# Storing the second attention's query and key parts in another layout, two key heads in the projection and the others from inside the attention

## The reference, cut to what matters

```
qkv = x @ Wqkv                                        # x: 2 x 1024 x 128
q = qkv[..., :256].reshape(B, 32, S, 8)               # 32 query heads of 8 features
k = qkv[..., 256:320].reshape(B, 8, S, 8)             # 8 key heads
v = qkv[..., 320:].reshape(B, 8, S, 8)
scores = q @ k.T / sqrt(8), masked causally, softmax  # 4 query heads share one key head
```

## Time and profile before

| | us |
|---|---|
| median of 3 runs (lowest, highest) | 3863.41 (3859.98, 3866.43) |
| the profiled execution, its own time | 3872.14 |
| its span, first to last instruction | 3870.2 |
| PE busy | 3113.8 |
| DVE busy | 2241.5 |
| ACT busy | 2093.1 |
| POOL busy | 1068.2 |
| mean granted TensorE clock | 0.899 |

### The profile page before, as it was taken

The page is one execution under the profiler, slowest core; times in us unless marked ns, Lnnn a source line. Parts: engine busy times, 40 slices in busy tenths (PEclk is TensorE's granted clock), DMA queues, the critical chain, the costliest instruction groups (busy, mean ns, idle before and its releaser), DMA issues. The chain is left out here.

```text
span 3870.2 us, 73056 instructions
## 1 busy us (share of the span) xinstructions
PE 3113.8 (80%) x24437; PEld 1669.6 (43%) x24437; DVE 2241.5 (58%) x3754; ACT 2093.1 (54%) x3805; POOL 1068.2 (28%) x967
## 2 busy tenths in 40 slices
PE   2787885279505999991999999999999999999997
PEld 1332331123201333331565566556556556655653
DVE  6888886732415777775555555555554554555553
ACT  1477775012201666660666666666666666666664
POOL 0000000024102111111554344344344434434540
PEclk7689778589755999995999999999999999999998
DMA  5221113034271111114111111111111111111111
GB/s 192 86 76 59 64 63 102 1 82 107 43 37 22 26 25 25 25 25 125 41 52 33 46 37 48 40 44 47 30 50 38 47 40 40 51 30 50 41 34 40
DMA packets 191919, 199.74 MB, mean 52 GB/s; under 512 B 113781, under 2 KB 120581, under 8 KB 186794
## 3 DMA queue, kind: packets, MB, share of 16 engines
q1 hardware_dynamic: 154218, 193.05, 18.1%
q10 hardware_dynamic: 37344, 1.97, 1.0%
HBM read 99.64 MB, written 28.97 MB: 33 GB/s over the span
## 5 line engine op out<-in xcount | busy, mean ns | idle before, releaser
L2398 POOL TENSOR_TENSOR tr_t<-tr_t 128x512 f32<-128x512 f32 x384 | 488.4, 1272 | 705.8 <-DVE tr_t L2242 705.8
L2405 POOL TENSOR_TENSOR tr_nq<-tr_t,tr_rn 128x512 f32<-128x512 f32 x384 | 392.2, 1043 | 395.2 <-ACT tr_rn L2138 395.2
L1610 DVE TENSOR_REDUCE attn_mp<-attn_ps 128x1 f32<-128x512 f32 (+3 forms) x660 | 395.6, 657 | 163.7 <-PE attn_ps L1461 86.5
L2103 ACT ACTIVATE tr_pr<-tr_ps 128x768 f32<-128x768 f32 x264 | 213.9, 810 | 375.1 <-PE tr_ps L1925 374.8
L2241 DVE TENSOR_TENSOR tr_t<-tr_ps,tr_tab 128x512 f32<-128x512 f32 x384 | 263.4, 686 | 242.7 <-ACT tr_sq L2112 242.6
L1940 PE MATMUL tr_ps<-tr_w,tr_xs 128*128 128x512 f32 x768 | 371.2, 605 | 32.1 <-DVE tr_xs L2269 27.9
L1572 ACT ACTIVATE attn_pr<-attn_ps 128x768 f32<-128x768 f32 (+2 forms) x352 | 300.9, 870 | 168.4 <-PE attn_ps L1494 165.5
L2251 DVE TENSOR_TENSOR tr_o<-tr_ps,tr_rd 128x384 f32<-128x384 f32 (+1 forms) x264 | 144.1, 546 | 427.8 <-ACT tr_rd L2128 426.9
L684 DVE TENSOR_REDUCE attn_mcol<-attn_ps 128x1 f32<-128x512 f32 x548 | 358.1, 683 | 46.3 <-PE attn_ps L529 36.7
L668 ACT ACTIVATE attn_pr<-attn_ps 128x512 f32<-128x512 f32 x512 | 272.7, 600 | 88.6 <-DVE attn_ps L706 69.0
L1925 PE MATMUL tr_ps<-tr_qT,tr_kT 64*128 64x96 f32 (+1 forms) x4224 | 300.9, 282 | 0.0
(11 more groups left out here) (260 smaller groups left out, 4947.3 us busy)
## 6 DMA issues: line engine op xcount, KB each, us to landing
tr_v<-tr_va SPq DMA_DIRECT2D x144, 192.0 KB, 2.5
attn_ka<-scratch_kp SPq DMA_DIRECT2D x72, 294.0 KB
tr_v<-tr_va SPq DMA_DIRECT2D x144, 128.0 KB, 2.4
moe_cb<-scratch_combineT SPq DMA_DIRECT2D x32, 512.0 KB
tr_w<-in_w_half SPq DMA_DIRECT2D x12, 1024.0 KB
tr_v<-tr_va SPq DMA_DIRECT2D x48, 256.0 KB, 2.4
scratch_kp<-proj_parts SPq DMA_DIRECT2D x36, 256.0 KB
attn_km<-scratch_kp SPq DMA_DIRECT2D x72, 98.0 KB
```

Of the source, the lines that this page charges most:

```text
L1610: dve.tensor_reduce(dst, src, AX.X, ALU.max).then_inc(maxed, 1)
L2398: pool.tensor_tensor(t12[:, slot, i, 0, :], t12[:, slot, i, 0, :], t12[:, slot, i, 1, :], ALU.add).then_inc(summed, 1)
L2405: pool.tensor_tensor(nq[:, slot, i, :].rearrange("p (h e) -> p h e", e=DH), t12[:, slot, i, 0, :].rearrange("p (h e) -> p h e", e=DH), rn[ ...
```

## The change

The layout of the scratch tensors changes: a key head's 128 tokens are now kept as pieces of 128 tokens (256 bytes), ordered by feature group. `move_q` writes one key head's query parts of one column tile by three DMAs, `move_k` its key parts by three, so nine DMAs (`MOVES`) write one key head. The projection writes heads 0 (SP) and 1 (ACT queue) only. `parts` lives on through the attention, with 512 columns of zeros behind its 2048 tokens; the attention's SP writes heads 2 and 3 before its loop and head `kv + 4` in iteration `kv`, and loads head `kv + 3` there (the third head, 2, before the loop), after the first output store. The stores of ones in `stage_masks` go. The loads of queries read rows of 32 pieces of 128 bytes where they read one run of 4 KB. POOL's copies read the new order. ACT's two copies of the output sums move from after a = 4 and a = 15 to after a = 3 and a = 14.

```diff
 def stage_masks
-            for h in range(2):
-                sp.dma_start(d["k1"][:, :, B * NK1 + h, :]...)
-            for h in range(2 * QPK):
-                sp.dma_start(d["q1"][:, :, B * NQ1 + h, :]...)
-            sp.wait_ge(stored, 16 * (3 + 2 * QPK))
+            sp.wait_ge(stored, 16)
+AHEAD = 4
+FIRST = 2
+MOVES = 9
+def move_q(eng, d, parts, kv, ct, signal):
+    for part in range(3):
+        dst = d["q1"][part, :, bass.ds(kv, 1), ct * 16 * P:(ct + 1) * 16 * P]
+        eng.dma_start(dst.rearrange("e o (c t) -> c e (o t)", t=P), parts[:, ct, part, bass.ds(kv * P, P)]
+                      ).then_inc(signal, 16)
+def move_k(eng, d, parts, kv, signal):
+    for part in range(3):
+        dst = d["k1"][part, :, bass.ds(kv, 1), :]
+        eng.dma_start(dst.rearrange("e o (c t) -> c e (o t)", t=P), parts[0:NK1 * HD, 2, part, bass.ds(kv * P, P)]
+                      ).then_inc(signal, 16)
 def stage_project1        # SP; the ACT queue the same with head 1
             for ct in range(2):
                 sp.wait_ge(split_done, ct + 1)
-                n += store_q(sp, ct, range(0, 8), stored)
+                move_q(sp, d, parts, 0, ct, stored)
             sp.wait_ge(split_done, 3)
-            n += store_k(sp, range(0, 4), stored)
-            sp.wait_ge(stored, 16 * n)
+            move_k(sp, d, parts, 0, stored)
+            sp.wait_ge(stored, 16 * MOVES)
...
             dve.memset(vaug[:], 1.0).then_inc(ones_ready, 1)
+            dve.memset(parts[:, :, :, T:], 0.0)
 def stage_attention1      # SP
-                    heads = bass.ds(kv * QPK + 2 * half, PAIRS)
-                    n += load_packed(sp, qh[halves[half], slot % 2], d["q1"][:, :, heads, :], QPART1, loaded[slot])
+                    heads = d["q1"][:, :, bass.ds(kv, 1), :].rearrange("a e o (c x) -> a e (o c) x", x=P)
+                    n += load_packed(sp, qh[halves[half], slot % 2], heads[:, :, :, 64 * half:64 * half + 64], QPART1,
+                                     loaded[slot])
...
             load(1, 1)
+            for kv in range(FIRST, AHEAD):
+                for ct in range(2):
+                    move_q(sp, d, parts, kv, ct, moved[kv % 2])
+                move_k(sp, d, parts, kv, moved[kv % 2])
+            sp.wait_ge(turned, 5)
+            sp.wait_ge(moved[0], 16 * MOVES)
+            load(2, 2)
...
-                    sp.wait_ge(qk_done, kv * UNITS + 1)
-                    load(kv + 2, (s + 2) % 4)
                     sp.wait_ge(out_copied, 2 * kv + 1)
                     store(QPK * kv + 1, 0)
+                    sp.wait_ge(turned, 5 * kv + 10)
+                    sp.wait_ge(moved[(s + 1) % 2], 16 * MOVES * (2 * i + (s + 3) // 2))
+                    load(kv + 3, (s + 3) % 4)
+                    for ct in range(2):
+                        move_q(sp, d, parts, kv + AHEAD, ct, moved[s % 2])
+                    move_k(sp, d, parts, kv + AHEAD, moved[s % 2])
                     sp.wait_ge(out_copied, 2 * kv + 2)
                     store(QPK * kv + OROW, 1)
 # POOL: the same five copies per head (turn_piece), reading the new order, at HEADS_AT = 8 of its list
-                                 kp[:, slot % 2, :].rearrange("p (j c t) -> p j t c", c=8, t=16)
+                                 kp[:, slot % 2, :].rearrange("p (c j t) -> p j t c", c=8, t=16)
-                        src = qh[:, slot % 2, p, :].rearrange("p (c m o t) -> p o m c t", c=32, o=2, t=4)
+                src = qh[:, slot % 2, :, :].rearrange("p c (h m o t) -> p h o m c t", h=2, o=2, t=4)
 # ACT
-                        if a == 4:
+                        if a == 3:
                             copy_out(2 * kv, 0, kv)
-                        elif a == 15:
+                        elif a == 14:
                             copy_out(2 * kv + 1, 1, kv)
 SCRATCH
-    "q1": ([3, HD, (B * NK1 + 2) * QPK, S], BF16),
-    "k1": ([3, HD, B * NK1 + 2, S], BF16),
+    "q1": ([3, HD, B * NK1 + AHEAD, QPK * S], BF16),
+    "k1": ([3, HD, B * NK1 + AHEAD, S], BF16),
```

More of the change, by code:

```diff
@@ L1091, in _, with stage_project1 @@
             dve.tensor_copy(negmask[:], m[:])
-def stage_project1(nc, d, xnT, vaug):
+AHEAD = 4
[11 more added lines that the diff above has]
+                      ).then_inc(signal, 16)
+def stage_project1(nc, d, xnT, vaug, parts):
     with Stage(nc, "proj1") as st:
         w = st.sb("w", [P, 2 * D + 2 * NK1 * HD])
-        parts = st.sb("parts", [P, 3, 3, T], BF16)
         r0, r1, r2 = st.sb("r0", [P, 3, T]), st.sb("r1", [P, T]), st.sb("r2", [P, T])
@@ L1111, in stage_project1 @@
         NV = NK1 * HD
[L1113 to L1129, removed]
         @block.sync
@@ L1177, in _ @@
                     k += 1
-            n = 0
             for ct in range(2):
                 act.wait_ge(split_done, ct + 1)
-                n += store_q(act, ct, range(8, 16), copied)
+                move_q(act, d, parts, 1, ct, copied)
             act.wait_ge(split_done, 3)
-            n += store_k(act, range(4, 8), copied)
-            act.wait_ge(copied, 16 * n)
+            move_k(act, d, parts, 1, copied)
+            act.wait_ge(copied, 16 * MOVES)
         @block.vector
@@ L1189, in _ @@
             dve.memset(vaug[:], 1.0).then_inc(ones_ready, 1)
+            dve.memset(parts[:, :, :, T:], 0.0)
             for j, rows in enumerate((P, P, NV)):
                 dve.wait_ge(mm_used, NC * (j + 1))
-                split_parts(link, dve, r0[0:rows, j, :], parts[0:rows, j, 0, :], parts[0:rows, j, 1, :],
-                            parts[0:rows, j, 2, :], r1[0:rows, :], r2[0:rows, :])
+                split_parts(link, dve, r0[0:rows, j, :], parts[0:rows, j, 0, 0:T], parts[0:rows, j, 1, 0:T],
+                            parts[0:rows, j, 2, 0:T], r1[0:rows, :], r2[0:rows, :])
                 dve.sem_inc(split_done, 1)
@@ L1215 @@
 LEAD_STEPS = 8
+HEADS_AT = 8
 PAIRS = 2
@@ L1294, in unit_index, with stage_attention1 @@
     return pos if pos < STEP_POS[T_STEP] else pos - 1
-def stage_attention1(nc, d, vaug, ident, identb, negmask):
+def stage_attention1(nc, d, vaug, parts, ident, identb, negmask):
     NKH = B * NK1
@@ L1303, in stage_attention1 @@
     with Stage(nc, "attn1") as st:
-        qh = st.sb("qh", [P, 2, PAIRS, S], BF16)
+        qh = st.sb("qh", [P, 2, 32, PAIRS * 32], BF16)
         kp = st.sb("kp", [P, 2, S], BF16)
@@ L1324, in stage_attention1 @@
         pool_begun = st.sem("pool_begun")
+        moved = [st.sem("moved0"), st.sem("moved1")]
         block = st.block()
@@ L1378, in _, with turn_keys, turn_queries, turn_piece @@
             for slot in range(4):
-                sp.wait_ge(loaded[slot], 16 * NLOAD * (NKH // 4 + (1 if slot < 2 else 0)))
+                sp.wait_ge(loaded[slot], 16 * NLOAD * (NKH // 4 + (1 if slot < 3 else 0)))
+            for x in range(2):
+                sp.wait_ge(moved[x], 16 * MOVES * (NKH + AHEAD - FIRST) // 2)
         @block.gpsimd
         def _(pool):
-            def turn_heads(slot):
+            def turn_keys(slot):
                 pool.tensor_copy(kh[:, slot, :].rearrange("p (j t c) -> p j t c", t=16, c=8),
-                                 kp[:, slot % 2, :].rearrange("p (j c t) -> p j t c", c=8, t=16)).then_inc(turned, 1)
-                for p in range(PAIRS):
-                    for c in range(2):
-                        src = qh[:, slot % 2, p, :].rearrange("p (c m o t) -> p o m c t", c=32, o=2, t=4)
-                        pool.tensor_copy(qt[:, slot, p, c * 4:c * 4 + 4, :].rearrange("p m (c t) -> p m c t", t=4),
-                                         src[:, c]).then_inc(turned, 1)
+                                 kp[:, slot % 2, :].rearrange("p (c j t) -> p j t c", c=8, t=16)).then_inc(turned, 1)
+            def turn_queries(slot, p, c):
+                src = qh[:, slot % 2, :, :].rearrange("p c (h m o t) -> p h o m c t", h=2, o=2, t=4)
+                pool.tensor_copy(qt[:, slot, p, c * 4:c * 4 + 4, :].rearrange("p m (c t) -> p m c t", t=4),
+                                 src[:, p, c]).then_inc(turned, 1)
+            def turn_piece(slot, i):
+                if i == 0:
+                    turn_keys(slot)
+                else:
+                    turn_queries(slot, (i - 1) // 2, (i - 1) % 2)
             def copy_values(kv, slot):
@@ L1403, in _ @@
                 pool.wait_ge(loaded[slot], 16 * NLOAD)
-                turn_heads(slot)
+                for x in range(5):
+                    turn_piece(slot, x)
             copy_values(0, 0)
@@ L1413, in _ @@
                             copy_values(kv + 1, (s + 1) % 2)
-                        if a == 10:
+                        if a == HEADS_AT:
                             pool.wait_ge(loaded[(s + 2) % 4], 16 * NLOAD * (i + 1 + (1 if s >= 2 else 0)))
                             pool.sem_inc(pool_begun, 1)
-                            turn_heads((s + 2) % 4)
+                            for x in range(5):
+                                turn_piece((s + 2) % 4, x)
         @block.tensor
```

10 lines of the change are left out of this document (3 added, 7 removed).

## The result

The changed kernel takes 3755.44 us (3748.00 to 3762.12, four runs) against 3864.92 (3859.98 to 3875.91, four runs): a ratio of 0.9712, 95% interval 0.9684 to 0.9741, 109.5 us less. The forecast was 3750 us, 113.5 us less.

The account below looks back on a forecast made before the run. Stores, through their number of pieces, bound an idle 96.7 us stretch; in the attention's loop PE is busy and waits for ACT's copy. Terms -4.05, -92, +0.5 and -18 give 113.5 us less: 3750 us, range 3738 to 3778.

Parts of the forecast that it names:

- Masks: Masks stage: ten stores go, so the next stage's load goes out 4.05 us sooner (3.8 to 4.3).
- Projection: Projection's end: 120 stores in 73,728 pieces give way to 18 stores; the attention starts 92 us sooner (90.9 to 93.6).
- Padding memset: Zeros behind the tokens in the projection: 4.1 us on DVE, costing nothing because DVE stands idle 14.29 us there.
- First loads: Attention's start: load 0 now reads 3072 pieces of 128 bytes; +0.5 us, bounds 0 to 5.9.
- SP's budget: Attention's loop: loads and moves before the second store take 10.1 us of 14.6 allowed, so PE does not wait.
- M: SP's nine moves in a head of the attention's loop: 4.0 us taken, from 3.0 to 6.2.
- signs of being right: Listed profile signs, among them SP idle before its second store and no PE wait for the row maxima's DMA.
- The copies: Attention's loop: ACT's two earlier copies remove PE's waits of 1.24 us a head; 18 us saved, at most 19.8.
- rival B: Attention's loop: PE's waits only move to the later exponential or DVE's maxima; 3768 us, chance 0.17.
- C: Attention's loads: small pieces at 2.87 ns hold up SP, rows 2.6 us late a head; 3797 us, chance 0.07.
- E: Projection's end held by something other than piece count, such as a fixed store cost; 20 us tail gives 3770, chance 0.03.
- D: Attention's two-part query loads run on few DMA engines, making the kernel slower than before; 3941 us, chance 0.03.

Follow-up runs that it names:

- the run with whole rows: First mention: kernel before, its 120 stores writing rows as 4 KB runs, 3785.73 us; second: changed kernel, loaded query rows contiguous 4 KB runs, 3751.55 us.

## Why the prediction was right

- *Masks.* Right in mechanism, and nearly in size: 4.4 us for 4.05, just over the upper bound of 4.3. SP's last issue ends as forecast, and the tail behind it is 1.70 us instead of 2.05.
- *Projection.* Right. The stores bounded an idle stretch, and it went but for 5.0 us, within the forecast of 3.3 to 6.0. Its two parts came out otherwise than I took them: the three key moves take 2.0 us on SP and 2.9 on the ACT queue, not 1.1, and the tail behind the last of them (1067.99 to 1070.04) is 2.05 us, the lower of my two. That pieces and not DMAs or bytes set the old time was read off two rows with the same 2.9 ns a piece; the run with whole rows shows it. With the moves of all heads in the stage the bound turns into 0.65 to 0.73 us an issue.
- *Padding memset.* Hidden as forecast; its price was 1.98 us, not 4.1.
- *First loads.* The term was mis-sized: +1.9 us for +0.5, within its bounds (0 to 5.9). I took the rate of the value load and let the pieces vanish under the issue time; the run with whole rows gives the 2.0 us to the pieces.
- *SP's budget.* The way of working was right, but that the rows stayed nearly in time was partly luck. M was mis-sized: the nine moves take 7.3 to 8.3 us with their gaps (4.0 forecast, 6.2 as upper bound), since no row of before had a DRAM side of 16 by 8. The loads take 6.5 us on average, not 6.1. From the first load to the second store it is 14.1 to 15.8 us, on average 14.6, which is just the limit that I had worked out; nothing is left of a margin of 4.5 us. Two of the forecast's signs of being right failed with it: SP is not idle before its second store, and PE waits for the row maxima 5 times, 2.3 us in all. In each of these five PE goes on 1.1 us after the end of SP's last row issue, so the landing takes less than the 2.0 us I had allowed. What makes the rows late is that SP issues them late: in four of those heads the second store took 2.2 or 3.0 us, where a usual one takes 1.8, and in the fifth the row issues took 3.6 instead of 2.8. The twelve heads are 3.1 us longer for it than 12 times 29.01.
- *The copies.* Right, and under-sized: forecast 18 us, measured 23.9 alone and 20.6 with the moves in the loop. A head fell by 1.38 us and not by the 1.24 of PE's waits, which the profile shows too short; the turns got shorter as well. So the loop's forecast came near by two errors against each other: 5.9 us too little for the copies, 3.3 us for late rows left out. The fear that the wait would move to the next exponential (rival B) did not come true: PE has no such wait.
- *Rivals.* C holds in kind and not in price: the pieces cost load 0 2.0 us for 5.9, and a head's loads 0.6 us of SP for 2.7. E is out with the tail of 2.05 us. D is out: loads issue at 0.32 us apiece, and from 1087 to 1091 us, with nothing but loads in flight, the 16 engines were 90% busy, where two are one eighth. The Trainium skill's rule on the number of engines (page "DMA: Bandwidth & Descriptors", section "Why a DMA increments its semaphore by 16 and not by 1"), on which D leaned, costs nothing here; whether that is because part and row dimensions are merged first, as the prediction supposed, no run shows.

The terms sum to 113.5 forecast and 116.2 in the profiles; the medians say 109.5 with an interval of some 11 us either way.

## What to carry to other kernels

Divide a store's time by its number of contiguous pieces before anything else: two rows with the same nanoseconds a piece and different bytes say that the pieces set the time, and that a layout with fewer of them is what to try. Once pieces are few, the issue is the price, and it goes onto whichever queue takes the work; put such issues where that queue has slack before its next deadline, and take their price from a row with the same walk on the DRAM side, or keep a wide margin. And a copy out of the one buffer that the next group of matmuls waits for should sit at the first point where its condition holds, even if it delays the engine's own next step, as long as nobody waits for that step; here nobody did.

## What was not expected of the hardware

- An issue of a DMA from SP costs 0.57 us with a DRAM side that walks 16 by 8 rows of 256 bytes, and 0.34 us when the same 128 rows lie one behind the other; 0.30 us for 8 rows of 4 KB. How the pattern is written in the source (a dimension of size 1 or not) changes nothing.
- One memset of 2304 four-byte elements on each of 128 partitions took 1.98 us, 0.86 ns an element: the 4608 bf16 zeros were written two at a time.
- A turn of the hardware loop adds 3.6 to 5.5 us over an ordinary head, and this scatters by up to 1.7 us within one execution (34.5, 33.1 and 32.8 us with all the moves in the projection).
